# Gate projection of half the rows from high and low parts; self-attention scores issued in halves among the projection's steps

## The reference

```python
def _L0_attn_ref(...):            # first layer: 4 heads of 64
    q, k, v = (silu(causal_dwconv(x @ W)) for W in (W_q, W_k, W_v))
    beta = sigmoid(x @ W_b)
    delta_out = delta_rule_chunkwise(q, k, v, beta)      # one chunk of 32 rows for each batch
    fir_s, fir_l = causal_dwconv(v, short), causal_dwconv(v, long)
    gate_in = concatenate([x, fir_s, fir_l, delta_out], -1)          # 1024 features
    hid = gelu(gate_in @ W_fuse1 + b_fuse1)                          # 512 features
    logits = (hid @ W_fuse2 + b_fuse2).reshape(b, l, H, 4)
    p_raw = sigmoid(logits[..., 3])
    others = softmax(logits[..., :3] / exp(others_log_tau), -1)
    o = mix of fir_s, fir_l, delta_out and v by these gates
    return rmsnorm(o, norm_w) @ W_o

def _L1_attn_ref(...):            # second layer: 16 heads of 64, keys shared by 4
    q, k, v = projections; q, k = rope(rms_norm(q)), rope(rms_norm(k))
    attn = softmax(q @ k.T, -1)
    return (attn @ v) @ Wo.T
```

## Time and profile before

| | us |
|---|---|
| median of 3 runs | 1607.41 |
| the three runs | 1605.9, 1607.41, 1612.63 |
| profiled execution | 1609.45 |
| its span, first to last instruction | 1607.6 |
| PE busy | 1484.7 (92%) |
| DVE busy | 1097.5 (68%) |
| ACT busy | 813.4 (51%) |
| POOL busy | 586.0 (36%) |

### The profile page before, as it was taken

How to read it: one execution, slowest core, us unless ns; L and a number is a source line. 1 busy time by engine, 2 the same in 40 slices (tenths; PEclk the granted TensorE clock), 3 DMA queues, 4 the chain that set the end, 5 groups by cost and what they waited for, 6 DMA issues and landing times. The chain is left out here.

```text
span 1607.6 us, 38476 instructions
## 1 busy us (share of the span) xinstructions
PE 1484.7 (92%) x15176; PEld 1139.9 (71%) x15176; DVE 1097.5 (68%) x2412; ACT 813.4 (51%) x1849; POOL 586.0 (36%) x487
## 2 busy tenths in 40 slices
PE   6898989999988889999999889999899788999998
PEld 4454467555456579999998756666688686799997
DVE  4588879973057455566562568888699676767887
ACT  1234742121134336666563548999377322766663
POOL 2440310000011035677654256787388452121210
PEclk9999999999999999999999999999999998999999
DMA  9992059522023367677657417664000000010001
GB/s 321 359 342 74 1 180 215 125 62 46 1 96 122 112 216 253 220 255 253 246 183 189 131 50 245 207 205 135 28 1 1 24 24 15 1 34 21 27 1 53
DMA packets 114075, 203.99 MB, mean 127 GB/s; under 512 B 38074, under 2 KB 74362, under 8 KB 108010
## 3 DMA queue, kind: packets, MB, share of 16 engines
q1 hardware_dynamic: 91481, 107.72, 23.0%
q0 software_dynamic: 10032, 57.55, 10.4%
q10 hardware_dynamic: 12384, 36.27, 6.8%
HBM read 161.67 MB, written 39.83 MB: 125 GB/s over the span
## 5 line engine op out<-in xcount | busy, mean ns | idle before, releaser
L2390 POOL TENSOR_TENSOR a_pr<-a_pr,a_inv 128x1028 f32<-128x1028 f32 x64 | 122.1, 1908 | 58.7 <-DVE a_inv L2523 58.6
L386 PE MATMUL ps<-kv_ctx,kv_w 128*128 128x257 f32 x464 | 120.6, 395 | 9.5 <-PEq L1841 3.1
L2485 ACT ACTIVATE a_pr<-ps,a_neg 128x257 f32<-128x257 f32 x256 | 119.0, 473 | 18.9 <-DVE a_neg L2539 18.8
L390 PE MATMUL ps<-kv_w,kv_ctx 128*128 128x256 f32 x464 | 114.4, 390 | 12.1 <-ACT kv_kv L410 11.5
L1631 POOL TENSOR_TENSOR b0m_pm<-b_dr,b_gates 128x256 f32<-128x256 f32 x16 | 13.2, 831 | 280.5 <-SPq L1595 251.5
L2539 DVE TENSOR_REDUCE a_neg<-ps 128x2 f32<-128x514 f32 x128 | 87.8, 688 | 37.4 <-PE ps L2407 36.4
L390 PEld LDWEIGHTS ps<-kv_w,kv_ctx 128*128 128x128 f32 x464 | 86.7, 193 | 32.3 <-ACT kv_kv L410 20.1
L3401 DVE SCALAR_TENSOR_TENSOR x<-ps,g_gate,x 128x256 f32<-128x256 f32 x256 | 105.1, 475 | 0.0
L386 PEld LDWEIGHTS ps<-kv_ctx,kv_w 128*128 128x128 f32 x464 | 85.5, 195 | 27.5 <-issue 15.0
L972 DVE SCALAR_TENSOR_TENSOR b_F<-b_F,b_fir 128x992 f32<-128x992 f32 (+29 forms) x128 | 96.5, 789 | 0.0
L2418 PE MATMUL ps<-ident,a_pr 128*128 128x128 f32 x512 | 80.4, 279 | 16.0 <-ACT a_prT L2492 10.6
(11 more groups left out here) (448 smaller groups left out, 4431.6 us busy)
## 6 DMA issues: line engine op xcount, KB each, us to landing
late_kv<-kv SPq DMA_DIRECT2D x52, 513.0 KB, 4.1
kv<-kv_kv ACTq DMA_DIRECT2D x46, 513.0 KB
a_ctxT<-in_ctxT SPq DMA_DIRECT2D x32, 514.0 KB, 8.8
a_ctxR<-in_ctx SPq DMA_DIRECT2D x32, 512.0 KB
kv_ctx<-in_ctxT ACTq DMA_DIRECT2D x34, 257.0 KB
kv_ctx<-in_ctxT SPq DMA_DIRECT2D x24, 257.0 KB
outs<-f_yo SPq DMA_DIRECT2D x16, 256.0 KB
a_vB<-vlast SPq DMA_DIRECT2D x32, 128.0 KB
```

The source lines that it names most:

```text
L386: done = e.matmul(out[:, 0:NK], self.w[:, 0, c, cols(part)], ctx[:, c, :], start=(c == 0), stop=(c == DC - 1))
L390: done = e.matmul(out[:, cols(t, D)], ctx[:, c, cols(t)], self.w[:, 1, c, :], start=(c == 0), stop=(c == DC - 1))
L2390: e.tensor_tensor(pr[:, b % RP, :, :], pr[:, b % RP, :, :], inv[:, b % 2, :].unsqueeze(2).to_broadcast([P, HG, NK]), ALU.mult).then_inc(*p ...
L2485: e.activation(pr[:, b % RP, r, :], K.ps[:, bank(b, r), 0:NK], ACT.Exp, bias=neg[:, b % 2, r:r + 1], accum_out=tot[:, b % 2, r:r + 1]).the ...
```

## The change

Three edits.

**Gates.** Groups 2 and 3 of the first projection (the second half of the rows) go by `product3` over high and low parts. The weights' high parts are made on ACT (8 copies, between the takings of the last eight pieces of keys ahead of the first `half_outputs`), their low parts on DVE (8 subtractions in place of the plain weights, once groups 0 and 1 are done). Each of the 16 input chunks is split by one copy on ACT (`high_source`) and one subtraction on DVE (`low_source`) into one of two places. The order of loops is turned: chunk outside, the four column blocks inside, four banks open at a time. Two pieces of keys move from before group 0 to after group 1. `qk` becomes `qq` and `kk`, so that new tiles can lie where `kk`, half of `xnT` and the plain weights were.

**Ends of the delta rule's blocks.** In the first block PE's piece of keys behind `norms(3)` goes ahead of it, ACT's two takings ahead of `normed(3)`, and DVE's `norms(3)` ahead of the first reciprocal. In the gates, exp of tau and its reciprocal go to the end of `delta_solve`, and the sigmoid becomes exp(-x), plus 1, reciprocal (the last two on DVE).

**Self-attention.** On PE step t is now weigh(t-3), then the eight steps of project(t-4), with the first half of scores(t) behind its third step and the second half behind its sixth. The wait for the banks of the scores stands ahead of the first half. Scores use banks 0 and 1 (tile 1: 2 and 3), the projection banks 2 and 3. On DVE the order of a step is exponents(t), transpose(t-1), low parts(t-2), addition(t-4), sums(t).

```diff
@@ first block of delta_attention: PE, ACT, DVE
                     norms_back(2)
-                    A.pe(e, 2)
+                    A.pe(e, 3)
                     norms(3)
-                    A.pe(e, 1)
                     norms_back(3)
...
-                    A.act(e, 1)
+                    A.act(e, 2)
                     normed(3)
-                    A.act(e, 1)
                     e.wait_ge(*v_n.at(NG - 1))
...
                     norms(2)
+                    norms(3)
                     e.wait_ge(*a_root.at(1))
                     e.reciprocal(rn[:, 0:12, :], rn[:, 0:12, :]).then_inc(*v_inv.up())
-                    norms(3)
@@ delta_solve
+        def low_weights(e, k):
+            if k == 0:
+                e.wait_ge(*a_wh.at(8))
+                e.wait_ge(*t_h.at(8))
+            e.tensor_tensor(f1L[:, k, :], f1[:, k, :], f1H[:, k, :].bitcast(F32), ALU.subtract).then_inc(*v_wl.up())
+
+        def low_source(e, n):
+            high, low = part(n)
+            e.wait_ge(*a_sh.at(n + 1))
+            e.tensor_tensor(low, source(n % 8, 2 + n // 8), high.bitcast(F32), ALU.subtract).then_inc(*v_sl.up())
...
+                def fuse_parts(first, last):
+                    for n in range(first, last):
+                        g, k = 2 + n // 8, n % 8
+                        e.wait_ge(*v_sl.at(n + 1))
+                        if g == 2:
+                            e.wait_ge(*v_wl.at(k + 1))
+                        for m in range(4):
+                            if k == 0:
+                                e.wait_ge(*a_h.at(4 * g + m - 3))
+                            done = product3(e, K.ps[:, m, :], [w[:, k, cols(m)] for w in (f1H, f1L)], part(n), k == 0, k == 7)
...
-                ahead.pe(e, 14)
+                ahead.pe(e, 12)
                 fuse_most(0)
                 ahead.pe(e, 8)
...
-                ahead.pe(e, 4)
-                fuse_most(2)
+                ahead.pe(e, 6)
+                fuse_parts(0, 6)
                 ahead.wait_taken(e)
                 half_outputs(1)
                 e.wait_ge(*v_o.at(NT))
                 logits(0)
-                fuse_rest(2)
-                fuse_most(3)
-                fuse_rest(3)
+                fuse_parts(6, 16)
                 logits(1)
@@ ACT
-                ahead.act(e, 50)
+                ahead.act(e, 40)
+                e.wait_ge(*ld_f.at(16))
+                e.wait_ge(*t_G.at(NT))
+                for k in range(8):
+                    e.activation(f1H[:, k, :], f1[:, k, :], ACT.Copy).then_inc(*a_wh.up())
+                    ahead.act(e, 1)
...
+                hidden(0)
+                hidden(1)
+                high_source(0)
+                high_source(1)
+                ahead.act(e, 6)
...
+                for n in range(6, 9):
+                    high_source(n)
+                hidden(2, (0, 1))
+                high_source(9)
+                hidden(2, (2, 3))
+                for n in range(10, 16):
+                    high_source(n)
+                hidden(3)
                 e.wait_ge(*t_lg.at(2))
                 e.activation(lgraw, K.ps[:, 4, :], ACT.Copy).then_inc(*a_raw.up())
+                e.activation(tau[:, :], ltau[:, :], ACT.Exp).then_inc(*a_tau.up())
@@ self_attention: PE
-                def project(t):
...
+                def project_and_scores(u, t):
+                    if u >= 0:
+                        e.wait_ge(*v_o.at(2 * u + 2))
+                        if u >= 2:
+                            e.wait_ge(*v_x.at(u - 1))
                     for c in range(8):
...
+                        if 2 <= t < NT:
+                            if c == 2:
+                                e.wait_ge(*v_sb.at(t))
+                            for n in {2: range(4), 5: range(4, 8)}.get(c, ()):
+                                done = scores_part(e, t, n)
...
-                for t in range(NT + 3):
-                    if 2 <= t < NT:
-                        scores(t)
...
+                for t in range(2, NT + 4):
+                    if 3 <= t < NT + 3:
+                        weigh(t - 3)
...
+                    project_and_scores(t - 4, t)
@@ DVE
-                for t in range(NT + 3):
-                    if 1 <= t <= NT:
-                        sums(t - 1)
-                    if 2 <= t <= NT + 1:
-                        low(t - 2)
+                for t in range(NT + 4):
                     if 2 <= t < NT:
                         exponents(t)
                     if 1 <= t <= NT:
                         turned(t - 1)
-                    if t >= 3:
-                        residual(t - 3)
+                    if 2 <= t <= NT + 1:
+                        low(t - 2)
+                    if t >= 4:
+                        residual(t - 4)
+                    if t < NT:
+                        sums(t)
```

143 lines of the change are left out of this document (87 added, 56 removed).

## The result

| | before | after | ratio, 95% interval |
|---|---|---|---|
| median, first chip | 1609.85 | 1586.61 (1580.33 to 1592.1) | 0.9848 (0.9812 to 0.9885) |
| median, second chip (as e9, below) | 1608.73 | 1592.28 (1586.34 to 1600.17) | 0.9894 (0.9859 to 0.9929) |
| profiled execution | 1609.45 | 1586.79 | |
| its span | 1607.6 | 1585.0 | |

The account below looks back on a forecast made before the run. PE (92% busy) mostly bounds it, with engines meeting at block ends and instruction-fetch waits in self-attention. 1609.45 - 8.5 - 1.5 - 3.4 - 8.5 = 1587.5 profiled; median 2.0 lower, 1585.5 us; eight in ten 1577 to 1596.

Parts of the forecast that it names:

- -10.1 by parts: Gates: three products of parts at 0.233 us replace a 0.858 us fp32 matmul, saving 0.158 x 4 blocks x 16 chunks.
- +0.7 for the hand-over and the change of groups: Gates: 0.7 us charged for a first hand-over and about 0.5 us waiting at the third block; ends 0 and 2.5.
- Rival A: Gates: splitting binds, ACT and DVE late for each chunk; part 1 worth 10 us less, 1595.5 us; chance 0.11.
- Outputs 3.5 sooner, of it -2.0 here: Gates' outputs: 3.5 us earlier, 1.5 from the first block's end, -2.0 here, limited by the solved matrices' loads.
- Part 2, the ends: -1.5 and -3.4: Delta rule: first block ends 1.5 us sooner by reordering; gates' block 3.4 sooner without table loads, key takings following PE.
- Work a step 5.34: Self-attention: two more detours between matmul shapes add 0.38 us to PE's 4.96 a step, giving 5.34.
- What the waits are: Self-attention: PE's pieces of about 250 instructions, fetched once the one before is begun, take 3.4 to 3.7 us.
- That the halves keep the waits away, and that this is the gain: Self-attention: products amid the scores limit fetch waits to 1.2 us, 0.2 a step; 5.54 instead of 5.93 us.
- Clock: Self-attention: only the first low-clock stretch returns, +1.3 us; swings were seen only after waits of 1.7 us and more.
- Rival B: Self-attention: mean fetch rate binds, 5.9 us a step, winning only 0 to 3; 1591 to 1595 us; chance 0.17.
- Rival C: Self-attention: runs at DVE's 4.95 us a step, winning 15.5 instead of 8.5; 1578.5 us; chance 0.13.
- Rival D: Self-attention: PE's stops keep the granted clock at 1.2 GHz, making the kernel slower, 1620 us; chance 0.03.

Follow-up runs that it names:

- e9: The kernel after, unchanged, six executions on the second chip: median 1592.28 us, 0.9894 of the kernel before.
- e3: Kernel before with self-attention's q and k tile in bf16, 240 instead of 368 instructions a step: 1603.45 us (before beside it 1606.69).
- e10: Kernel before plus 32 small fp32 matmuls (128 instructions) ahead of the self-attention's pipeline, shifting the instruction pieces: 1634.86 us (before beside it 1628.99).
- e11: Kernel before, unchanged, traced a second time: 1613.41 us (before beside it 1628.99).
- e2: Kernel after with the scores' first half directly behind the weighing, the second behind the projection's fourth step: 1590.91 us (before beside it 1606.69).
- e4: Kernel after with 14 and 4 pieces of keys around the gates' first groups instead of 12 and 6: 1584.15 us (before beside it 1606.69).
- e1: Kernel after with all 64 score matmuls in one piece behind the projection's third step: 1595.57 us (before beside it 1606.69).
- e7: Kernel after with two instead of four clock matmuls ending the first block, and 16 and 2 pieces of keys: 1586.3 us (before beside it 1610.88).
- e5: Kernel after with all 64 score matmuls directly behind the weighing, later weighing and other banks kept: 1592.18 us (before beside it 1610.88).
- e6: Kernel after with scores in quarters behind the projection's third, fourth, sixth and seventh step: 1589.5 us (before beside it 1610.88).
- e8: Kernel after with 14 and 4 key pieces, two first-block clock matmuls, self-attention's clock matmuls behind tile 2's scores: median 1585.29 us, 0.9843 of before.

## Why the prediction was right

The time was right (1586.6 for 1585.5), and the four parts came out near their terms: by means over the traces that share the code -8.9, -1.7, -2.3 and -7.4 where -8.5, -1.5, -3.4 and -8.5 were forecast, together -20.3 for -21.9. Within them several steps were off and cancelled, and that the median hit to 1.1 us is luck: the same kernel's six executions on the second chip have a median of 1592.3.

**Part 1, gates: -8.5.** From the first Gram matrix to the last logits the four traces with the old gates (before, e3, e10, e11) took 231.4, 231.1, 228.5 and 229.4 us, the six with 12 and 6 pieces 217.9 to 223.0, mean 221.3 against 230.1: -8.9. The pair of profiled executions alone has -11.7. (Read by the trace's own clock the outputs came at 329.1 and 396.4 and the transposes at 440.3, where 326.5, 393 and 438.5 were foretold; the 4.1 us by which this execution was late beforehand cover it.)
- *-10.1 by parts*: right. Products at 0.233; logits(0) to the last logits 34.7 instead of 41.1 (40 of the 64 matmul groups, -6.4 where 6.3 were due), chunks 0 to 5 -3.7 where 3.8 were due.
- *+0.7 for the hand-over and the change of groups*: too high. PE waited 0.2 in all, and the change of groups cost 0.1. Rival A did not happen: within a group ACT stands idle 1.8 to 2.1 us ahead of a split.
- *+2.9 for the pieces behind group 1*: 2.7 (-1.3 before them, +1.4 at the first part).
- *Outputs 3.5 sooner, of it -2.0 here*: this step failed. From the first Gram matrix they came 1.1 sooner on the mean (112.3 to 111.1), and from trace to trace anything from 3.2 sooner (e9) to 0.2 later (e2). I let the matrices' loads move with the block's start and gave them 2.2 to 4.3 us to land. But the path begins with DVE's last step of solving and a store, and the term left out what the keys' transfers on ACT do to that store: 2.6 us from its issue to the loads' where they keep off, 5.1 to 5.2 where they fall on it (e4); the waits at the outputs were 3.0 us in after, 6.3 in e2 and 6.9 in e1.

**Part 2, the ends: -1.5 and -3.4.** The first block's end came 1.7 us sooner, counted from 200 us, and that in every trace (16.9 us to the first Gram matrix in the four old ones, 15.2 in the new ones with four clock matmuls), with DVE's work over at 217.96 and PE last, by its clock matmuls, as said; e7 shows the 1.03 us that they cost. The gates' block went from -9.2 to -12.6 in the pair (-3.4), the table's 0.5 in the block before it was there (the block began 1.98 us after the logits' transposes instead of 1.51), and nothing else was late. But this is the better case of two. From the transposes to `delta_mix` the old traces took 9.6 to 10.8 us, mean 10.3, the new ones 7.5 in six and 9.1 in three (e2, e5, e6), mean 8.0: -2.3. In the three the keys' matmuls there took up to twice as long (the eight of L390 3.58 us in e5, 1.89 in after), with a granted clock of 0.72 from 438 to 444 us in e5 where after has 1.00 in its place. PE had been idle for 0.70 and 1.32 us just before, in the good traces too; in before, where it was 0.70 and 0.85, the clock is 1.00 there and falls only at 456.8 us. That the longer idle time is to blame is not shown.

**Part 3, self-attention: -8.5.** Measured from 1200 us to the last addition -8.0 in this pair and -7.4 on the means of two traces of before and four of after's order; by the loop -7.5 in the pair, and 95.9 against 88.9 on the means: -7.0. A step was 5.50 on the mean of eleven where I had 5.54.
- *Work a step 5.34*: 5.43. The excursion was under-priced: the first cut costs 0.34, since half of the scores lasts 0.68 and not 0.61.
- *Waits 0.2 a step*: 0.07.
- *What the waits are*: right in the main, and sharper than put: every 256th instruction is where PE can wait. The detail that a piece is fetched only when the one before is begun is wrong in 19 to 30 cases a trace; packets at least 3.3 us apart fit all of them.
- *That the halves keep the waits away, and that this is the gain*: this step's conclusion fell. They keep them away, but e1, with the scores whole, has them back and is as fast. Some 4 of the 7 us come from parting the scores from the weighing (e5); in the three traces of before's loop (before, e10, e11) and in e5, where these stand together, gaps of 2 us and more and low stretches in mid-loop were seen, and in no other; the largest elsewhere is 1.3. The other 2.8 are not separated from the pieces' position (e10).
- *Clock*: of the three low stretches of the earlier trace rows one was left, at the loop's start, as charged. In before it fell behind waits of 2.4 and 1.7 and did not behind two of 1.9 and 1.8 (1284.25, 1327.89), in e5 it fell behind one of 1.8 and in e10 behind one of 1.44; in e1 behind none of up to 1.2. So the length of the last wait alone does not decide it, and the prediction's line at 1.7 does not hold.
- *Rival B* (the mean counts, not the burst) fell in its number, 5.9 a step, but not wholly in its idea: four orders of the same 368 instructions all ended within 1.3 us. 368 instructions are 1.44 pieces, at 3.4 to 3.9 us 4.9 to 5.6 us a step (an estimate; at the shortest spacing of packets, 3.3 us, it is 4.8), which may be why orders with less work of PE's own gain nothing. *Rival C* would have needed DVE's 4.95, below most of that band. *Rival D*: the clock did not stay low.

The last words of the prediction asked for no move over 2 us outside the three stages; there were two, +4.1 and -2.5, and the second trace of before shows moves of that size with no change at all.

## What to carry to other kernels

Where a loop of small matmuls shows waits for "issue", number PE's records, semaphore waits among them: if the waits lie a multiple of 256 apart, count how long each 256 instructions last and part the densest groups by long matmuls. Cutting them finer gained no more here (e6); fewer instructions took every such wait away (e3). Clock-keeping matmuls are worth placing like work: behind the first dense group instead of ahead of it they took two waits for issue away, though a wait for DVE took the place of one (e8). Before work is moved along the program, see which transfers move with it: two pieces of keys moved cost PE about what they saved, but ACT's transfers for them landed on a store that PE's next work waits for.

## What was not expected of the hardware

- PE's waits for issue of over half a microsecond in this loop stand at numbers 193 + 256 k of its records in every trace that has such waits, also with 8 instructions less or 128 more ahead of it.
- One packet of 16 KB is fetched for each 256 records, at least 3.3 us after the last one and at least 2.2 us ahead of its first instruction, and never for more than two pieces ahead.
- Half of the scores (64 records) takes 0.68 us up to the next product, a quarter 0.28, the whole 1.22: the price of a cut depends on the size, and finer cuts were cheaper than the first.
- The same store of the solved matrices took 2.6 us until its loads were issued where no other transfer was started within 3 us of it, and 5.1 to 5.2 us where ACT had started one 0.4 to 1.2 us earlier.
- One and the same code ran at a granted clock of 1.00 or 0.72 in the gates' block, in six and in three executions.
